# Normalisation shared by VectorE and ScalarE, an earlier routing, and the weight splits taken off GpSimd, in an attention and expert layer

## What is computed

```python
xn = _layernorm(x)                       # over the 128 features
# attention part, within each block
s = xn @ W_spin.T + b_spin
g = mean(s, axis=1) @ W_global.T
scores = (s @ W_J.T) @ s.T / sqrt(128)
a = tanh(beta * (s + g + softmax(scores) @ s))
# expert part: 16 experts, the two best for each token
logits = xn @ Wg.T + bg ; top_vals, top_idx = top_k(logits, 2)
cw = softmax(top_vals) spread over the experts by top_idx
gu = xn @ Wgu[e] + bgu[e] ; gate = min(gu[::2], 7) ; up = clip(gu[1::2], -7, 7)
out_e = ((up + 1) * gate * sigmoid(1.702 * gate)) @ Wd[e] + bd[e]
return x + a + sum_e(cw[e] * out_e)
```

## Time and profile before

| what | us |
|---|---|
| median of 3 runs | 385.84 |
| lowest and highest of them | 384.03 and 386.58 |
| the profiled execution | 387.06 |
| its span in the profile | 385.1 |
| step 0's exponential starts | 41.29 |
| first and last scatter of L448 start | 100.51 and 187.64 |
| first turn of slots on PE | 193.56 |
| first gather of L478 starts | 295.56 |

### The profile page before, as it was taken

The page is one execution under the profiler, slowest core; times in us unless marked ns, Lnnn a source line. Parts: engine busy times, 40 slices in busy tenths (PEclk is TensorE's granted clock), DMA queues, the critical chain, the costliest instruction groups (busy, mean ns, idle before and its releaser), DMA issues.

```text
span 385.1 us, 6131 instructions
## 1 busy us (share of the span) xinstructions
PE 345.9 (90%) x1833; PEld 284.2 (74%) x1834; DVE 294.6 (77%) x588; ACT 254.1 (66%) x517; POOL 213.0 (55%) x246
## 2 busy tenths in 40 slices
PE   2769899897999999999987999999999999999960
PEld 1647688565787788888867898999877887788830
DVE  4896976999978879878847677777757879976642
ACT  4945776664589687786754476766666687688720
POOL 4607796222677788777423243343322777777771
PEclk9997999999999999999998899999999999999985
DMA  5999500000011211212231344443323224334331
GB/s 135 335 316 388 192 0 2 0 4 26 21 55 56 76 51 40 79 49 80 75 98 29 94 128 119 131 136 110 109 59 90 56 60 123 76 83 101 84 82 41
DMA packets 37301, 36.48 MB, mean 95 GB/s; under 512 B 3812, under 2 KB 29028, under 8 KB 37276
## 3 DMA queue, kind: packets, MB, share of 16 engines
q1 hardware_dynamic: 33132, 27.70, 23.6%
q0 software_dynamic: 4144, 8.48, 8.3%
HBM read 19.27 MB, written 16.88 MB: 94 GB/s over the span
## 4 chain that ended last, share of the span: by engine, by line
POOL 35%; PE 31%; DVE 14%; issue 11%; DMA 3%; ACT 3%; SPq 1%; POOLq 0%; DVEq 0%; ACTq 0%
POOL slots_x L448 16%; POOL made L478 8%; PE PS L487 8%; POOL gy L478 8%; PE PS L489 7%; PE PS L488 7%; DVE mx L988 4%; PE PS L696 2%; PE PS L702 2%; PE PS L594 2%; DVE pl L973 2%; PE PS L541 1%; POOL rows L439 1%; POOL gu_sb L467 1%; PE PS L527 1%
## 5 line engine op out<-in xcount | busy, mean ns | idle before, releaser
L973 DVE TENSOR_TENSOR pl<-PS,ph 128x512 fp32r<-128x512 f32 x128 | 87.7, 686 | 31.2 <-ACT ph L842 30.5
L833 ACT ACTIVATE PS<-PS 128x512 f32<-128x512 f32 x128 | 74.8, 584 | 46.4 <-PE PS L489 44.9
L988 DVE TENSOR_REDUCE mx<-PS 128x1 f32<-128x512 f32 x128 | 84.3, 682 | 9.1 <-PE PS L541 8.8
L842 ACT ACTIVATE ph<-PS 128x512 fp32r<-128x512 f32 x128 | 76.6, 598 | 12.2 <-PE PS L489 0.4
L448 POOL DMA_INDIRECT slots_x<-xn,posu x64 | 62.4, 975 | 19.8 <-issue 18.9
L541 PE MATMUL PS<-xT,gq 128*128 128x512 f32 x128 | 48.4, 418 | 6.8 <-DVE mx L988 6.5
L487 PE MATMUL PS<-ph,rows 128*128 128x512 f32 x128 | 51.5, 403 | 3.2 <-DVE pl L973 3.1
L487 PE MATMUL PS<-gq,xT 128*128 128x512 f32 x128 | 52.5, 410 | 1.1 <-DVE pl L973 1.1
L467 POOL TENSOR_TENSOR gu_sb<-gu_sb 128x512 f32<-128x512 f32 x20 | 25.5, 1277 | 47.0 <-DVE gu_sb L1203 47.0
L489 PE MATMUL PS<-gq,xT 128*128 128x512 f32 x128 | 50.1, 391 | 0.0
L489 PE MATMUL PS<-ph,rows 128*128 128x512 f32 x128 | 50.0, 391 | 0.0
(11 more groups left out here) (179 smaller groups left out, 659.0 us busy)
## 6 DMA issues: line engine op xcount, KB each, us to landing
slots_x<-xs SPq DMA_DIRECT2D x1, 5120.0 KB, 21.8
xy<-slots_x SPq DMA_DIRECT2D x20, 256.0 KB, 2.9
slots_y<-xy SPq DMA_DIRECT2D x20, 256.0 KB, 2.3
xn<-in_L_attn_x SPq DMA_DIRECT2D x8, 256.0 KB, 5.2
w_f<-in_L_ffn_Wgu SPq DMA_DIRECT2D x1, 2048.0 KB, 13.5
late<-in_L_ffn_Wgu SPq DMA_DIRECT2D x1, 2048.0 KB, 19.0
xs<-in_L_attn_x SPq DMA_DIRECT2D x8, 256.0 KB, 3.3
out_y<-made SPq DMA_DIRECT2D x8, 256.0 KB, 2.5
```

Of the source, the lines that this page charges most:

```text
L833: A(S[:, n % 3], S[:, n % 3], ACT.Exp).then_inc(exp_done, 1)
L842: A(ph[:, i % RING], S[:, n % 3], ACT.Copy).then_inc(s_hi, 1)
L973: v.tensor_tensor(dst, S[:, n % 3], high.bitcast(F32), ALU.subtract).then_inc(s_lo, 1)
L988: v.tensor_reduce(mx4[:, a, c:c + 1], MX[:, n % 2], AX.X, ALU.max).then_inc(mx_free, 1)
```

## The change

- Chunks 0, 1, 3, 6 and 7 are normalised by DVE, chunks 2, 4 and 5 by ACT (4 and 5 in two halves each). For chunks 4 to 7 GpSimd works out scale and shift, with the power -0.5 in place of root and reciprocal (`scales`). GpSimd splits the tokens of block 0 only when all four chunks are normalised, and folds the weights only after chunk 7.
- The order of the prologue changes on every engine; idle products go from 4, 6 and 4 to 2, 2 and 2.
- The 8 halves of spins and logits of block 1 move from steps 2 to 9 to steps 1 to 5, three of which make two halves. Mean, global row and counts follow.
- Routing's pieces go from steps 10 to 29 to steps 6 to 22. Piece 6 counts tiles with three operations of 16 elements in place of a comparison and a sum over 512. The row of the mean is written by ACT.
- GpSimd no longer splits the expert weights: in steps 38, 40, ... 68 ACT casts one expert's 384 columns, and DVE subtracts in the step after. The low parts of block 1's rows go from GpSimd to DVE, in steps 36, 38, 40 and 42.

```diff
-        SPIN_AT = {2 + h: (1, h) for h in range(8)}
-        GLOBAL_AT = {11: 0, 13: 1}
-        COUNT_AT = {17: 0, 19: 1}
+        SPIN_AT = {1 + n: [(1, h) for h in hs] for n, hs in enumerate(((0,), (1, 2), (3, 4), (5, 6), (7,)))}
+        GLOBAL_AT = {8: 0, 10: 1}
+        COUNT_AT = {13: 0, 15: 1}
+
+        WEIGHT_AT = {38 + 2 * n: n for n in range(NE)}
+        ROW_LO_AT = {36 + 2 * c: c for c in range(CB)}
...
(GpSimd)
+            def scales(c):
+
+                n, q = c - CB, slice(4 * c, 4 * c + 4)
+                pool.wait_ge(dev_in, c + 1)
+                g.tensor_scalar(mv[:, q, 1], mv[:, q, 1], EPS, None, ALU.add).then_inc(var_up, 1)
+                g.tensor_scalar(mv[:, q, 0], mv[:, q, 0], -1.0, None, ALU.mult).then_inc(var_up, 1)
+                pool.wait_ge(var_up, 2 * n + 2)
+                g.tensor_tensor(rstd[:, q], mv[:, q, 1], nhalf[:], ALU.pow).then_inc(root, 1)
+                pool.wait_ge(root, n + 1)
+                g.tensor_tensor(shift[:, q], mv[:, q, 0], rstd[:, q], ALU.mult).then_inc(scale_ready, 1)
+
+            for c in range(CB):
+                pool.wait_ge(xn_ready[c], 1)
+            pool.wait_ge(consts, 14)
+            rows_of(0)
+            rows_of(1)
+            scales(4)
+            rows_of(2)
+            rows_of(3)
+            for c in range(5, NCH):
+                scales(c)
+            pool.wait_ge(xn_ready[NCH - 1], 1)
             pool.wait_ge(ld_e, 32)
...
-            pool.wait_ge(w_row, 16)
-            for k in range(4):
-                q = slice(k * NE // 4, (k + 1) * NE // 4)
-                g.tensor_copy(wh[:, q], w_f[:, q]).then_inc(w_hi, 1)
-                pool.wait_ge(w_hi, k + 1)
-                g.tensor_tensor(wl[:, q], w_f[:, q], wh[:, q].bitcast(F32), ALU.subtract).then_inc(w_lo, 1)
...
-                    for k in range(CB, NCH):
-                        t = 4 * (k - CB)
-                        pool.wait_ge(row_h[1], k - CB + 1)
-                        g.tensor_tensor(rows[1][:, 1, t:t + 4, 1:D], xn[:, TB + t:TB + t + 4, 1:D],
-                                        rows[1][:, 0, t:t + 4, 1:D].bitcast(F32), ALU.subtract)
...
(PE)
             turn_tokens(0)
-            turn_tokens(1)
             pe.wait_ge(bend_out, 1)
...
+            turn_tokens(1)
             turn_tokens(2)
             pe.wait_ge(h_cut, 1)
             queries(0)
-            idle_products(4)
+            idle_products(2)
             turn_tokens(3)
-            idle_products(6)
+            idle_products(2)
...
-            pe.wait_ge(w_lo, 4)
+            pe.wait_ge(w_lo, NE)
...
(ACT, the end of the prologue)
+            A(warm[:], epsc[:], ACT.Exp)
             spins_out(0, 0)
             spins_out(0, 1)
-            normalise(4)
-            deviation(6)
-            deviation(7)
-            A(warm[:], epsc[:], ACT.Exp)
             spins_out(0, 2)
+            normalise(4, 0, 2)
             spins_out(0, 3)
-            normalise(5)
+            normalise(4, 2, 4)
             queries_hi(1)
             spins_out(0, 4)
             spins_out(0, 5)
-            normalise(6)
+            normalise(5, 0, 2)
             spins_out(0, 6)
+            normalise(5, 2, 4)
             spins_out(0, 7)
...
+                if i in (7, 9):
+                    mean_out(i // 2 - 3)
...
+                if i in WEIGHT_AT:
+                    n = WEIGHT_AT[i]
+                    if n == 0:
+                        act.wait_ge(w_row, 16)
+                    A(wh[:, n], w_f[:, n], ACT.Copy).then_inc(w_hi, 1)
...
(DVE)
+            def normalise(c):
+                if c < CB:
+                    dve.wait_ge(rstd_ready, c + 1)
+                    for t in range(4 * c, 4 * c + 4):
+                        ins = v.tensor_scalar(xn[:, t, 1:D], xn[:, t, 1:D], rstd[:, t:t + 1], shift[:, t:t + 1], ALU.mult, ALU.add)
+                else:
+                    dve.wait_ge(scale_ready, c - CB + 1)
+                    for t in range(4 * c, 4 * c + 4):
+                        ins = v.scalar_tensor_tensor(out=xn[:, t, 1:D], in0=xn[:, t, 1:D], scalar=rstd[:, t:t + 1],
+                                                     in1=shift[:, t:t + 1].broadcast_to([P, D - 1]), op0=ALU.mult, op1=ALU.add)
+                ins.then_inc(xn_ready[c], 1)
...
-                v.tensor_scalar(mean_bc[:], ident[:], 0.0, xsum[:, b, CB:CB + 1], ALU.mult, ALU.add).then_inc(mean_ready, 1)
...
             tokens_lo(2)
-            inverse(4)
-            inverse(5)
-            for a in range(4):
-                maximum(0, a, a, 0)
+            for q in range(4):
+                maximum(0, q, q, 0)
+            moments(4)
             queries_lo(0)
             tokens_lo(3)
-            moments(6)
-            moments(7)
...
+            for q in range(4, 8):
+                maximum(0, q, q % 4, q // 4)
+            moments(5)
+            for q in range(8, 16):
+                maximum(0, q, q % 4, q // 4)
+            dve.wait_ge(consts, 13)
+            shifts(0)
+            queries_lo(1)
             moments(6)
             moments(7)
...
-                    link(v.tensor_tensor(KEY_E, bc(small[:, 0], flat, 2), bc(j128, flat, 1), ALU.is_gt))
-                    link(v.tensor_reduce(small[:, 1], KEY_E, AX.X, ALU.add))
+                    link(v.tensor_scalar(tiles_i[:], small[:, 0], float(P - 1), None, ALU.add))
+                    link(v.tensor_scalar(tiles_i[:], tiles_i[:], 7, None, ALU.arith_shift_right))
+                    link(v.tensor_copy(small[:, 1], tiles_i[:]))
...
-            ROUTE_AT = {10: 0, 12: 1, 13: 2, 15: 3, 17: 4, 18: 5, 19: 6, 20: 7, 22: 8, 24: 9, 25: 10, 27: 11, 29: 12}
+            ROUTE_AT = {6: 0, 8: 1, 9: 2, 11: 3, 12: 4, 14: 5, 15: 6, 16: 7, 17: 8, 19: 9, 20: 10, 21: 11, 22: 12}
...
+                if i < 2:
+                    normalise(6 + i)
...
+                if i in ROW_LO_AT:
+                    c = ROW_LO_AT[i]
+                    t = 4 * c
+                    dve.wait_ge(row_h[1], c + 1)
+                    v.tensor_tensor(rows[1][:, 1, t:t + 4, 1:D], xn[:, TB + t:TB + t + 4, 1:D],
+                                    rows[1][:, 0, t:t + 4, 1:D].bitcast(F32), ALU.subtract).then_inc(row_l[1], 1)
+                if i - 1 in WEIGHT_AT:
+                    n = WEIGHT_AT[i - 1]
+                    dve.wait_ge(w_hi, n + 1)
+                    v.tensor_tensor(wl[:, n], w_f[:, n], wh[:, n].bitcast(F32), ALU.subtract).then_inc(w_lo, 1)
```

110 lines of the change are left out of this document (52 added, 58 removed).

## The result

| | kernel before | kernel after |
|---|---|---|
| median (range), us | 386.57 (383.75 to 386.94, 10 runs) | 388.44 (387.03 to 389.94, 10 runs) |
| ratio to the kernel before | 1 | 1.0087, 95% interval 1.0062 to 1.0112 |
| profiled execution, us (span) | 387.06 (385.1) | 387.33 (385.6) |

What follows compares the result with a forecast made beforehand. PE's stream was taken as the bound, GpSimd's only 0.7 us later at step 78. Steps to 32 (-3.5), steps 36 to 69 (+2.0) and PE's wait (-0.7) gave -2.2 us: 383.6 us, range 379.5 to 389.5.

Steps and rivals of the forecast that it cites:

- X(i): Start of ScalarE's exponential that marks attention step i; the forecast cut the span into stages at these points.
- Prologue, -3.0: Before the attention steps: VectorE's normalising and the new order bring the first low part 3.0 us earlier, at 39.8.
- Steps 2 to 5, +3.8: X(2) to X(6): three more spin halves cost 2.0 us, waits for bank E 1.8 us.
- Steps 6 to 23, 36.9 us: X(6) to X(24), early routing with VectorE as the bound: takes 36.9 us, X(24) 2.0 us earlier.
- X(24) to X(32), 14.3: Eight steps without routing's last pieces go at PE's pace: 14.3 us instead of 15.8.
- Steps 36 to 69, +2.0: Subtractions added to VectorE and casts to ScalarE fit on average but not step by step: 2.0 us lost.
- PE's wait at step 78, -0.7: Ahead of the expert section: GpSimd's slots come early enough to save PE's 0.7 us wait.
- From step 78 to the end "keeps its length": Expert section, gathers and everything behind move with steps 78 and 79, their length unchanged.
- Rival 1: Steps 36 to 69: the additions hide, or the early part gains more; 381.0 us, chance 0.26.
- Rival 2: PE's clock falls ahead of step 2, costing 2.5 us net in steps 2 to 5; 386.1 us, chance 0.20.
- Rival 3: Steps 36 to 69: VectorE becomes the bound, subtractions waiting for scatters, 5 to 8 us lost; 390 us, chance 0.12.
- Rival 4: Nothing gained on the path: spins' waits and added work eat the early gain; 385.8 us, chance 0.07.

Runs made afterwards that it cites:

- e3: Changed kernel with one half of the spins in each of steps 1 to 8 and routing in steps 9 to 28; 492.5 us on a chip that stopped (before 484.7).
- f2: The same kernel as e3, run again on another chip; 385.06 us, ratio 0.9979 to the kernel before.
- e5: Changed kernel with routing pieces 4 and 6 and ScalarE's routing exponential moved to other steps; 496.5 us on a chip that stopped (before 484.7).
- g2: f2 plus idle products in step 1 (nine) and the expert section (six and four); 383.99 us, ratio 0.9944 to the kernel before.
- j1: g2 with the moved weight cuts and row subtractions put in steps where the kernel before leaves VectorE room; 381.00 us, ratio 0.9875 to the kernel before.
- h3: Changed kernel with idle products in step 1 and the expert section, nothing else; 500.9 us on a chip that stopped (before 488.3).
- i2: The same kernel as h3, run again; 495.5 us on another chip that stopped (before 488.9).
- f4: Kernel before with only the change's weight cuts and row subtractions on ScalarE and VectorE in steps 36 to 69; 388.03 us, ratio 1.0073.

## Why the prediction was wrong, step by step

The sum was -3.5 + 2.0 - 0.7 = -2.2. By X(i) and the slots' turn it came out as 0.0 + 3.3 - 0.7 = +2.6, and the turn is indeed 2.5 us late. **Two terms failed: the 36.9 us of steps 6 to 23, which were 39.1, and the 2.0 us lost in steps 36 to 69, which were 3.3.** The 3.5 us that were missing at X(32) are 0.8 up to X(2), 0.7 in steps 2 to 5 and 2.2 in steps 6 to 23, less 0.2 behind them.

- **Prologue, -3.0: right** for the first low part, 39.97 (39.8). First maximum 18.79 (18.5), shift 34.05 (33). Sizes inside were off and cancelled in part: a chunk's four passes take 1.11 us, not 0.9, the power 1.05 us, not "nothing", the bias 0.21 where 0.3 was said. But X(2) gained only 2.2. The change puts one half of the spins into step 1, and on PE its six products stand between the first low part and step 2's scores (from 41.42 to 42.09, 0.67 us). The forecast counted the seven halves behind X(2) and left this one out.
- **Steps 2 to 5, +3.8: about right.** X(2) to X(6) grew by 4.5; e3 and f2 give 4.1 to 4.2 of it to the three added halves, 1.4 each where the sum took 0.68 and 0.6. X(6) was 1.5 late against the forecast, half of it from X(2).
- **Steps 6 to 23, 36.9 us: wrong by 2.2.** This is the step that broke the early gain. VectorE was rightly named as bound (37.9 us busy of 39.1), but its work was counted too small. Before, VectorE was busy for 29.1 of the 30.2 us between X(10) and X(24); with the forecast's own additions (5.3 + 2.7 - 1.3) that makes 35.8 us, 2.1 less than was measured. The sum added durations from places where nothing interfered. Two one-input passes stood beside a GpSimd addition and took 0.81 and 0.77 us instead of about 0.17 (e5):

```profile
74.02 1.28 POOL L436 TENSOR_TENSOR xs<-late 128x512 bf16<-128x512 f32 x1 [2.73 <-DVE late L1123]
...
74.53 0.81 DVE L1126 TENSOR_SCALAR mk<-mk 128x32 f32<-128x32 f32 x1
...
80.02 1.30 POOL L439 TENSOR_TENSOR late<-late 128x512 f32<-128x512 f32 x1 [4.72 <-DVE late L1134]
...
80.59 0.77 DVE L1137 TENSOR_SCALAR tiles_i<-late 128x16 int32<-128x16 f32 x1
```

  That is 1.2 us, of which e5 got 0.85 back in the stage's length. Where the other 0.9 us of VectorE's work comes from stays open. ScalarE's 2.6 us wait in step 10 is in no term either, and rightly so: the scores came no sooner.
- **X(24) to X(32), 14.3: right** (14.08). But it started 3.7 us later than forecast, so X(32) gained nothing. That X(32) is equal to the hundredth in both kernels is a coincidence: f2, g2 and j1 have it at 109.0 to 110.4.
- **Steps 36 to 69, +2.0: right mechanism, 1.3 too small.** The first pile-up was right: 2.2 forecast for the steps to 43, and X(36) to X(46) is 2.01 longer. X(46) to X(58) lost 0.16, where 0.5 was said. The term failed in two ways: the third stretch, X(58) to X(70), lost 1.08 and had no line in the sum, and nothing was "given back at the idle ends". Durations were near (549 ns a weight subtraction, 680 a row subtraction), and VectorE's busy time grew by 8.1 us, less than the 10.1 of the forecast: the size of the work was not what failed, but how it meets the crowded steps. And the term had no part for the 1.9 us by which PE's own busy time grew behind its waits.
- **PE's wait at step 78, -0.7: right**, the wait is gone.
- **From step 78 to the end "keeps its length": wrong for the profiled pair.** X(78) to X(80) is 93.30 in the profile of before and 89.63 in that of after, where the clock fell less; X(80) to X(90) takes 21.69 and 23.27, since in after it fell in 292 to 296 (granted 0.57); behind X(127) after takes 0.8 us less (17.4 and 18.2). The two fastest executions of after (387.0 and 387.3) had a mean granted clock of 0.972, the three slowest (389.5 to 389.9) 0.957 to 0.965. These falls are, as far as the rows show, most of why the pair of profiles shows 0.3 us and the medians 1.9. The medians' 1.9 is less than the 2.5 at the turn; how the 0.6 divides was to be told by h3 and i2 and is not settled.

**The rivals.** Rival 1 (the additions hide, 381.0) is the opposite of what happened, and j1 shows that it was a matter of place. That j1 took just 381.0 is chance, for about half of its gain comes from useless products, which rival 1 knew nothing of. Rival 2 (clock ahead of step 2) was real, 1.8 us in four of the eight profiled executions with the 2.40 us wait left open, 0.5 to 0.6 in three, and nothing in the one profiled of after. Rival 3 predicted the right side by the wrong mechanism: 16 subtractions with two SBUF inputs ran among the scatters at 549 ns each, where 0.56 was estimated for one that waits for nothing, and f4 shows the same loss with other scatters beside it. The group of after:

```profile
L1227 DVE TENSOR_TENSOR wl<-w_f,wh 128x384 fp32r<-128x384 f32 x16 | 8.8, 549 | 0.2 <-ACT wh L916 0.2
```

Rival 4 was the nearest in mechanism, though not in size (385.8): the spins' waits and the half in step 1 ate part of the early gain, early routing the rest, and the added work took more than was left. Its chance of 0.07 was too small.

The forecast's own sentence that work "fits on average but not step by step" was the key to the loss, and should have been worked out for every step from 6 to 78 instead of for two stretches.

## What to carry to other kernels

Work that is moved onto an engine beside the bounding one is to be placed by that engine's idle time in each step, not in equal distances: the same 36 instructions cost 3.4 us every other step and 0.55 where the step had room. An engine's early start is worth what the most crowded later stage lets through. A long wait in a list is no cost by itself: ScalarE's 2.6 us in step 10 cost nothing, as what it needed next came no sooner. And before a wait of PE like the 2.40 us here is called free, the granted clock behind it is to be read in several executions; a few idle products in it are cheap, and ten of them in the expert section gave the kernel before 0.6%.
